# GpSimd's masked gates in eight instructions, its decayed k in four, and one step of its order moved up by a chunk

## The reference

```python
def step(S, xs):
    qt, kt, vt, gt, bt = xs
    S = S * jnp.exp(gt)[..., None, None]
    kS = jnp.einsum('bhk,bhkv->bhv', kt, S)
    S = S + bt[..., None, None] * kt[..., :, None] * (vt - kS)[..., None, :]
    o = jnp.einsum('bhk,bhkv->bhv', qt, S)
    return (S, o)
```

## Time and profile before

| what | value |
|---|---|
| median of 3 runs | 2043.58 us (2041.25 to 2050.09) |
| the profiled execution's own time | 2045.8 us |
| its span, first to last instruction | 2043.7 us |
| PE busy | 1827.2 us (89%) |
| DVE busy | 1463.2 us (72%) |
| ACT busy | 995.1 us (49%) |
| POOL busy | 748.6 us (37%) |
| mean granted TensorE clock | 0.972 |

### The profile page before, as it was taken

The page is one execution under the profiler, slowest core; times in us unless marked ns, Lnnn a source line. Parts: engine busy times, 40 slices in busy tenths (PEclk is TensorE's granted clock), DMA queues, the critical chain, the costliest instruction groups (busy, mean ns, idle before and its releaser), DMA issues.

```text
span 2043.7 us, 43310 instructions
## 1 busy us (share of the span) xinstructions
PE 1827.2 (89%) x14658; PEld 1330.9 (65%) x14698; DVE 1463.2 (72%) x2413; ACT 995.1 (49%) x2742; POOL 748.6 (37%) x848
## 2 busy tenths in 40 slices
PE   4468886888799999999999999999999999999997
PEld 3236663333455678777777787777777877777776
DVE  5686773111457488888888888888888888888886
ACT  1002223777422255556556555565565555655654
POOL 5730002110030207256264372562643625626435
PEclk9789997999989999999999999999999999999999
DMA  6625662000013201010010110100101101001010
GB/s 250 213 78 186 203 190 78 21 21 11 29 57 93 93 7 42 0 41 29 12 41 0 41 41 0 41 32 9 41 0 41 41 0 41 36 5 41 0 62 21
DMA packets 75254, 111.75 MB, mean 55 GB/s; under 512 B 23318, under 2 KB 56742, under 8 KB 72006
## 3 DMA queue, kind: packets, MB, share of 16 engines
q1 hardware_dynamic: 71694, 102.32, 15.2%
q0 software_dynamic: 3072, 8.39, 1.3%
q10 hardware_dynamic: 446, 0.48, 0.1%
HBM read 85.80 MB, written 28.52 MB: 56 GB/s over the span
## 4 chain that ended last, share of the span: by engine, by line
PE 54%; DVE 8%; ACT 5%; issue 5%; POOL 1%; DMA 0%; DVEq 0%; ACTq 0%; SPq 0%; POOLq 0%
PE ps L1298 9%; PE ps L1336 6%; DVE conv L1918 5%; PE ps L1479 3%; PE ps L1346 3%; PE ps L1577 3%; PE ps L1566 3%; PE ps L1457 3%; PE ps L1442 3%; PE ps L1579 2%; PE ps L1553 2%; PE ps L1519 2%; ACT gmask_Q L1717 2%; PE ps L1508 2%; PE ps L1558 2%
## 5 line engine op out<-in xcount | busy, mean ns | idle before, releaser
L1918 DVE SCALAR_TENSOR_TENSOR conv<-raw,tap_st,conv 128x1024 f32<-128x1024 f32 x202 | 324.3, 1605 | 3.6
L1298 PE MATMUL ps<-xnT,w_conv_st 128*128 128x512 f32 x544 | 247.9, 599 | 0.0
L1796 POOL TENSOR_TENSOR kq_decayed<-conv,decay_rows 128x256 f32<-128x256 f32 x238 | 183.8, 795 | 130.9 <-PE ps L1577 130.9
L816 DVE TENSOR_REDUCE m_part<-ps 128x1 f32<-128x640 f32 (+7 forms) x176 | 176.1, 1027 | 68.0 <-PE ps L667 50.3
L1765 POOL TENSOR_TENSOR gmask_Q<-upto,g 128x2048 f32<-128x2048 f32 x17 | 61.3, 3609 | 361.4 <-DVE conv L1927 331.3
L998 ACT ACTIVATE probs<-ps 128x1024 f32<-128x1024 f32 (+7 forms) x256 | 146.0, 661 | 58.3 <-PE ps L933 28.9
L1298 PEld LDWEIGHTS ps<-xnT,w_conv_st 128*128 128x128 f32 x544 | 99.0, 192 | 100.9 <-issue 96.4
L1598 ACT COPY raw<-ps 128x512 f32<-128x512 f32 x136 | 80.5, 592 | 149.3 <-PE ps L1298 148.5
L1346 PE MATMUL ps<-w_z_st,xnT 128*128 128x256 f32 x512 | 148.8, 393 | 0.0
L903 POOL DMA_INDIRECT slot_outputs<-scratch_slots_y,token_slots x32 | 30.5, 954 | 317.0 <-POOLq L496 207.7
L1025 DVE COPY oT<-ps 128x1024 f32<-128x1024 f32 x8 | 9.8, 1225 | 172.0 <-PE ps L920 172.0
(11 more groups left out here) (347 smaller groups left out, 4525.8 us busy)
## 6 DMA issues: line engine op xcount, KB each, us to landing
decay_rows<-scratch_egc SPq DMA_DIRECT2D x17, 1024.0 KB, 4.6
w_conv_st<-in_w_conv SPq DMA_DIRECT2D x17, 512.0 KB, 5.4
scratch_slots_x<-yacc SPq DMA_DIRECT2D x8, 1024.0 KB, 14.5
slot_rows<-scratch_slots_x SPq DMA_DIRECT2D x16, 512.0 KB, 4.8
scratch_slots_y<-slot_outputs SPq DMA_DIRECT2D x16, 512.0 KB, 3.8
w_gate_up<-in_gu SPq DMA_DIRECT2D x8, 768.0 KB
w_gate_up<-in_gu SPq DMA_DIRECT2D x32, 192.0 KB
k_nat_decayed<-in_gu SPq DMA_DIRECT2D x22, 256.0 KB, 2.7
```

The costliest lines, as they stand in the source:

```text
L816: dve.tensor_reduce(dst, src, AX.X, ALU.max).then_inc(s_max, 1)
L1298: mm = pe.matmul(ps[:, 6 + n % 2, :], wc[:, k, (n // 2) * P:(n // 2 + 1) * P], m.xnT[:, k, (n % 2) * HALF:(n % 2 + 1) * HALF], start=k == ...
L1796: op = g.tensor_tensor(kqe[:, e, :, at], cv[:, 0:2, at], egr[:, e, at].unsqueeze(1).broadcast_to([P, 2, P]), ALU.mult)
L1918: op = dve.scalar_tensor_tensor(out=cv[:, t, :], in0=raw[:, t, at:at + T], scalar=tap[:, t, at:at + 1], in1=cv[:, t, :], op0=ALU.mult, op1 ...
```

## The change

`gmask` writes the same 128x2048 product in eight instructions of 128x256 (two chunks each), with the semaphore on the last. The decayed k of each e is written in two instructions of 128x512, again with the semaphore on the last. And `scalars(i + 1)` is issued after `decayed(5)` instead of after `decayed(6)`.

```diff
             def gmask(r):
                 gsrc = m.g[:, 0:2, :] if isinstance(r, int) else m.g[:, bass.ds(2 * r, 2), :]
-                g.tensor_tensor(gm_q[:], m.upto[:].unsqueeze(1).unsqueeze(1).broadcast_to([P, 2, NC, P]),
-                                gsrc.unsqueeze(3).broadcast_to([P, 2, NC, P]), ALU.mult).then_inc(s_gm, 1)
+                for e in range(2):
+                    for c in range(0, NC, 2):
+                        op = g.tensor_tensor(gm_q[:, e, c:c + 2], m.upto[:].unsqueeze(1).broadcast_to([P, 2, P]),
+                                             gsrc[:, e, c:c + 2].unsqueeze(2).broadcast_to([P, 2, P]), ALU.mult)
+                op.then_inc(s_gm, 1)
...
                 for e in range(2):
-                    g.tensor_tensor(ke[:, e], knat[:], m.eg[:, 1, bass.ds(2 * i + e, 1), :].rearrange("p h c -> p (h c)").unsqueeze(2)
-                                    .broadcast_to([P, NC, P]), ALU.mult).then_inc(s_ke, 1)
+                    for half in range(2):
+                        of = slice(4 * half, 4 * half + 4)
+                        op = g.tensor_tensor(ke[:, e, of], knat[:, of], m.eg[:, 1, bass.ds(2 * i + e, 1), of].rearrange("p h c -> p (h c)")
+                                             .unsqueeze(2).broadcast_to([P, NC // 2, P]), ALU.mult)
+                    op.then_inc(s_ke, 1)
...
                     decayed(c)
-                    if c == 6:
+                    if c == 5:
                         pool.wait_ge(s_vn, i * 2 + 2)
                         pool.wait_ge(s_hm, i * 3 + 3)
                         scalars(i + 1)
```

## The result

| | before | after |
|---|---|---|
| median | 2042.67 us (2041.25 to 2050.09, 4 runs) | 2012.74 us (2011.3 to 2016.71, 4 runs) |
| profiled execution, its span | 2045.8, 2043.7 us | 2013.75, 2011.8 us |

The ratio is 0.985, with an interval of 0.9829 to 0.9871: 30 us or 1.5% faster. The chips that the experiments ran on differ by 1.6% in absolute time (the kernel before took 2010 to 2043 us on them), so experiments are told by their ratio to the kernel before on the same chip, and by the length of an iteration in the loop, from its first L1442 to that of the next. That length is the same to 0.02 us where two chips ran the same loop.

The account below looks back on a forecast made before the run. The prediction took PE to bound the loop, its largest wait being for DVE's copy of S. Gains of 28.8 + 0.8 = 29.6 us gave a forecast median of 2014.0 us, range 2008 to 2027.

Parts of the forecast that it names:

- What bounds the kernel, and the turns: In the loop PE bounds; DVE's convolution is shut out during GpSimd's long gate product, and whole instructions of the two alternate.
- Part 1: Gates in eight instructions: PE's 1.80 us wait at L1553 for DVE's copy of S vanishes, 28.8 us over 16 times.
- Part 2: Decayed k in four instructions: 0.8 us gained once, in the first iteration's head, bounds 0 and 1.67; otherwise 0.
- Part 3: Scalars a chunk sooner: GpSimd's tail up to 0.9 us later, within its free time, so cost 0.
- The slack of 1.7 us: Free time between GpSimd's last power in the tail and PE's need of DVE's result from it: 1.2 + 0.5 us.
- the rival about the tail: GpSimd's tail becomes the bound: a 2.7 us delay gives back 16 us, median 2030; chance 0.10.
- Starved DVE: GpSimd keeps access through all eight gate pieces, so DVE's convolution waits: 24 us slower, 2068; chance 0.04.
- Half of it, in chunk 1: DVE is busy in chunk 1, so L1553 or L1566 waits 0.5 us: 8 us less gain, 2022; chance 0.12.
- Doesn't do what it says: DVE's convolution L1918 was slow for another reason, such as its own operands: no gain, 2043.6; chance 0.03.
- The sum: Whole kernel: 28.8 + 0.8 = 29.6 us less, giving a median of 2014.0 us.

## Why the prediction was right, and where not

The median was forecast at 2014.0 us, 2008 to 2027, and is 2012.74. By its steps:

- **What bounds the kernel, and the turns.** Right, and shown rather than argued: the convolution follows the end of the first instruction in five lengths of it, the iteration follows too down to 1.90 us, and moving the long instruction by 1.6 us does what cutting it does. DVE gets its turn after one piece of eight.
- **Part 1, 28.8 us.** It gave 29.4 (16 x 1.84), 0.04 us an iteration more than the idle time in the row of L1553. The eight pieces with DVE's turns took 6.58 us, where I had 4.9 + 2 x 1.28 = 7.5: back to back a piece costs 0.57 us and not its 0.612, and a turn of DVE costs GpSimd 0.98 us (the longest piece, 1.597, less 0.612), not the 1.28 of DVE's instruction. GpSimd caught up by `decayed(2)`, a chunk earlier than allowed for. Chunk 1's convolution takes 1.72 us (0.44 for a piece), with 0.28 us of idle left before DVE's next row: cost 0, as taken.
- **Part 2, 0.8 us once.** The wrong-sized term: it gave 0.06 us. The pair in the first iteration fell from 4.23 to 4.04 us only, and the instruction before it, L1994 (L1988 before), grew from 1.26 to 1.40:

```profile
715.22 1.26 DVE L1988 SCALAR_TENSOR_TENSOR yacc<-X,yacc 128x1024 f32<-128x1024 f32 x1 [4.34 <-ACT X L1645]
```

```profile
713.77 1.40 DVE L1994 SCALAR_TENSOR_TENSOR yacc<-X,yacc 128x1024 f32<-128x1024 f32 x1 [4.34 <-ACT X L1645]
715.09 4.04 DVE L1924 SCALAR_TENSOR_TENSOR conv<-raw,tap_st,conv 128x1024 f32<-128x1024 f32 x2
```

Together they are 0.05 us shorter, and the first iteration fell by 0.06 us more than the others. Four half-length instructions take more turns between DVE's than two long ones did: what a shorter one saves DVE at first, the next one takes. That halving the length halves the wait holds for one instruction of DVE, not for a series of them. In the other iterations the four pieces gave 0, as forecast.
- **Part 3, 0.** Right: GpSimd's last power ends at 1201.83, 2.64 us before PE's L1325 at 1204.47; it was 2.91 before. The shift is 0.27 us where I had allowed 0.9: the two large instructions lost 0.98 and 0.97 us to DVE's pair, not all of its 2.61. The slack of 1.7 us was read for one reader alone. With `a_own` as the second, 1.66 us more of delay cost 1.33 us an iteration, so the rival about the tail was too cheap in my account: 16 us for a slip of 2.7 us, where 0.27 + 1.66 cost 22. That it didn't matter for the forecast is owed to the small slip, not to the account of the slack.
- **The rivals.** Starved DVE: out by the 1.52 us. Half of it, in chunk 1: out, for no wait of PE at L1553 is left. "Doesn't do what it says": out by the five lengths.
- **The sum.** The loop gave 29.4 + 0.06 us for the 29.6 forecast. That this is so close is partly luck: part 1 gave 0.6 more and part 2 0.7 less. The medians differ by 29.9, and their own spread is several us, so they can't tell more.

## What to carry to other kernels

When DVE's two-input instruction is several times its usual length, look which GpSimd instruction it overlaps: it waits until that one ends. What matters is how long the GpSimd instruction that is running still lasts when DVE's critical one asks; so put a short one, or none, at that place, by cutting off a short first piece or by one wait, and leave the rest long. And when an engine's slack is read from a trace, look for every reader behind it and at what its next instructions will collide with when they are late.

## What the runs showed that I had not expected

- A delay of GpSimd can grow on its way: 1.66 us of idle work put two instructions of 0.20 us under DVE's and made them 1.18 and 1.10 us.
- The granted clock can fall to its lower level for 3.4 us after PE waits of 1.8 us inside a loop that is otherwise at the full level: six times of 15 where a wait of 0.7 us followed close, once in 16 waits in the kernel with the decayed k in four alone, and not at all in the loop of the kernel before, which has the same 1.8 us wait 16 times. Why it falls in one iteration and not in the next is not shown. The fall costs 1.3 to 1.7 us each. The gain of the change in these traces holds none of it.
- A turn costs the one that waits less than the other's whole instruction: DVE's 1.28 us instruction delayed a GpSimd piece by 0.98 us, and a GpSimd piece of 0.61 us delayed DVE's by 0.24 to 0.44 us. DVE's instruction asks somewhere within the piece, and by its usual 1.28 us its own work begins 0.2 us before the piece's recorded end, in these traces for every length from 0.61 to 3.61 us.
